# A decoder layer on one core: rows of b2 loaded ahead and the slot outputs read back in four parts

## What is computed

```python
dispatch = softmax(logits, axis=1)                      # logits (B, N, E, S) = (8, 512, 16, 16)
combine = softmax(logits.reshape(B, N, E * S), axis=-1).reshape(B, N, E, S)
slot_in = einsum('bnd,bnes->besd', xn, dispatch)
h = gelu(einsum('besd,edh->besh', slot_in, w1) + b1[None, :, None, :])
slot_out = einsum('besh,ehd->besd', h, w2) + b2[None, :, None, :]
out = einsum('besd,bnes->bnd', slot_out, combine)
x = layernorm(x + out)
```

## Time and profile before

| | |
|---|---|
| median of 3 runs | 2111.36 us (2105.56 to 2112.68) |
| the profiled execution's own time | 2112.64 us |
| its span | 2110.9 us |
| PE busy | 1974.6 us (94%) |
| DVE busy | 1453.8 us (69%) |
| ACT busy | 1221.2 us (58%) |
| mean over the span of what the DMA engines moved | 95 GB/s |
| expert loop, first output copy to last store landed | 2010.23 to 2051.62 us |
| combining, first to last DVE sum | 2055.65 to 2106.4 us |

### The profile page before, as it was taken

One profiled execution on the slowest core, in us unless ns is written; L12 is line 12 of the kernel. 1 busy time (PEld: TensorE's weight loads), 2 busy tenths in 40 slices (PEclk: granted clock), 3 DMA queues, 4 the chain that ended last, 5 costly groups with the idle time before them and its releaser, 6 DMA issues. The chain is left out here.

```text
span 2110.9 us, 40225 instructions
## 1 busy us (share of the span) xinstructions
PE 1974.6 (94%) x13484; PEld 1328.5 (63%) x13484; DVE 1453.8 (69%) x2889; ACT 1221.2 (58%) x3068; POOL 390.2 (18%) x597
## 2 busy tenths in 40 slices
PE   7899999999999999858999999999999999889988
PEld 5667675768676767444565656656656655478853
DVE  7978787878787878526667575757575767556438
ACT  4435353534444444217878787878787787546614
POOL 1110101111111111231221222222222122100006
PEclk9999999999999999878999999999999999999999
DMA  7122222222222222242324343433333332631157
GB/s 215 49 69 70 60 79 60 79 60 79 55 83 50 89 50 68 80 125 63 109 70 118 76 122 81 121 81 102 93 102 96 88 98 73 180 133 61 60 188 270
DMA packets 120291, 200.72 MB, mean 95 GB/s; under 512 B 23072, under 2 KB 44576, under 8 KB 120096
## 3 DMA queue, kind: packets, MB, share of 16 engines
q1 hardware_dynamic: 110880, 179.20, 28.3%
q0 software_dynamic: 9216, 18.89, 3.6%
HBM read 117.27 MB, written 29.88 MB: 70 GB/s over the span
## 5 line engine op out<-in xcount | busy, mean ns | idle before, releaser
L1769 ACT ACTIVATE a_shared<-a_shared,a_mx 128x512 f32<-128x512 f32 x512 | 340.9, 669 | 57.3 <-DVE a_mx L1830 57.2
L1762 ACT ACTIVATE a_probs<-a_scores 128x512 f32<-128x512 f32 x512 | 291.7, 603 | 98.8 <-PE a_scores L1972 96.4
L1830 DVE TENSOR_REDUCE a_mx<-a_shared 128x1 f32<-128x512 f32 x512 | 318.4, 682 | 14.4 <-PE a_shared L1956 13.3
L1972 PE MATMUL a_scores<-a_qs,a_ks 98*128 98x512 f32 x512 | 218.9, 435 | 21.7 <-ACT a_probs L1762 17.4
L1956 PE MATMUL a_shared<-a_ks,a_qs 96*128 96x512 f32 x512 | 214.9, 431 | 18.9 <-ACT a_shared L1769 14.3
L939 PE MATMUL m_proj<-m_xt_hi,link 128*128 128x512 f32 x544 | 224.6, 413 | 6.3 <-DVE m_acc L652 6.3
L1094 PE MATMUL m_outp<-m_wout,m_g 128*128 128x512 f32 x512 | 225.2, 598 | 2.7 <-issue 2.7
L940 PE MATMUL m_proj<-m_xt_lo,link 128*128 128x512 f32 x544 | 215.4, 396 | 0.0
L941 PE MATMUL m_proj<-m_xt_hi,link 128*128 128x512 f32 x544 | 214.3, 394 | 0.0
L1930 PE MATMUL a_shared<-link 128*128 128x512 f32 x768 | 190.6, 401 | 18.9 <-POOL a_ks L1702 15.7
L467 ACT ACTIVATE m_acc<-m_proj,m_cb,m_cw 128x512 f32<-128x512 f32 x72 | 58.1, 817 | 257.5 <-PE m_proj L941 257.3
(11 more groups left out here) (266 smaller groups left out, 3487.7 us busy)
## 6 DMA issues: line engine op xcount, KB each, us to landing
m_dec<-step_decay SPq DMA_DIRECT2D x64, 256.0 KB, 4.1
a_qs<-link SPq DMA_DIRECT2D x256, 64.0 KB, 2.1
m_ce<-run_decay SPq DMA_DIRECT2D x128, 112.0 KB, 3.5
a_ks<-a_k_hi POOLq DMA_DIRECT2D x192, 64.0 KB, 2.4
e_x<-x SPq DMA_DIRECT2D x11, 1024.0 KB, 5.6
m_xt_in<-x_t_in SPq DMA_DIRECT2D x8, 1024.0 KB, 8.3
m_x_tok<-x_in SPq DMA_DIRECT2D x8, 1024.0 KB, 5.5
x<-m_x_tok SPq DMA_DIRECT2D x32, 256.0 KB, 2.2
```

The costliest lines, as they stand in the source:

```text
L1762: act.activation(probs[:, n % 2, h, :], scores[t.score_bank(n, h)][:, :], ACT.Exp, scale=-1.0).then_inc(exp_ready, 1)
L1769: act.activation(scored[:, :], scored[:, :], ACT.Exp, scale=-1.0, bias=mx[:, i % 2, j, h:h + 1], accum_out=den[:, i, j, h:h + 1]).then_inc ...
L1830: dve.tensor_reduce(mx[:, i % 2, j, h:h + 1], bank(what)[:, :], AX.X, ALU.min).then_inc(mx_ready, 1)
L1972: pe.matmul(scores[t.score_bank(n, h)][:, :], ks[0:STACK + 2, t.slot(i), h, j * P:(j + 1) * P], qs[0:STACK + 2, t.slot(i), h, :], start=Tr ...
```

## The change

`b2row` now holds the rows of all eight experts 8 to 15, loaded at the stage's start in two DMAs of 1 MB, each with its own semaphore (`b2_in[0]`, `b2_in[1]`), and no row is loaded inside the loop. The 2 MB read of the first half becomes four of 512 KB, each for two sequences. They stand behind the stores of experts 9, 10, 11 and 12; the first still waits for the stores of experts 0 to 7. Each part has a semaphore of its own, three of them taken over from loads that are long done. VectorE waits for part n before it adds the bias to pair n.

```diff
-B_PAIR = 2
 HALF = NE // ST_TILES
-FIRST_ROW = HALF // B_PAIR
...
-        b2row = sb("b2row", [P, 2, B_PAIR, DM])
+        b2row = sb("b2row", [P, HALF, DM])
...
+        slot_in = [(c_in[0], 16), (b2_in[0], 32), (b2_in[1], 32), (b2_slot_in, 16 * HALF + 16)]
...
-            def load_bias(c):
-                sp.dma_start(b2row[:, c % 2], b2[B_PAIR * c:B_PAIR * (c + 1)].partition_broadcast(P)).then_inc(b2_in[c % 2], 16)
...
-            for c in range(FIRST_ROW, FIRST_ROW + 2):
-                load_bias(c)
+            for n in range(2):
+                half = slice(n * HALF // 2, (n + 1) * HALF // 2)
+                sp.dma_start(b2row[:, half, :], b2[HALF:NE][half].partition_broadcast(P)).then_inc(b2_in[n], 16)
...
-                if e >= HALF and e % B_PAIR == B_PAIR - 1 and e // B_PAIR + 2 < NE // B_PAIR:
-                    load_bias(e // B_PAIR + 2)
-                if e == HALF + 1:
+                piece = e - HALF - 1
+                if piece == 0:
                     for n in range(SO_BUFS):
                         sp.wait_ge(so_out[n], 16 * HALF // SO_BUFS)
-                    load_slots(0, 0, n_seq, c_in[0])
+                if 0 <= piece < n_seq // 2:
+                    s, count = slot_in[piece]
+                    if piece:
+                        sp.wait_ge(s, count - 16)
+                    load_slots(0, 2 * piece, 2 * piece + 2, s)
...
-                    c = e // B_PAIR
-                    dve.wait_ge(b2_in[c % 2], 16 * ((c - FIRST_ROW) // 2 + 1))
+                    dve.wait_ge(b2_in[2 * (e - HALF) // HALF], 16)
                     dve.tensor_tensor(so[0:rows, e % SO_BUFS, :], out_bank(e)[0:rows, :],
-                                      b2row[0:rows, c % 2, e % B_PAIR, :], ALU.add).then_inc(so_ready, 1)
+                                      b2row[0:rows, e - HALF, :], ALU.add).then_inc(so_ready, 1)
...
                     if b == 0:
-                        dve.wait_ge(c_in[0], 16)
                         dve.wait_ge(b2_slot_in, 16 * HALF)
+                    dve.wait_ge(*slot_in[b // 2])
```

## The result

Over 19 runs of each, the changed kernel took 2105.31 us (median; 2098.73 to 2109.71) and the one before 2111.66 us. The ratio is 0.9972, with a 95% interval of 0.9965 to 0.998: about 5.9 us less, 4.2 to 7.4. Its profiled execution has a span of 2105.0 us, against 2110.9.

The account below looks back on a forecast made before the run. For 24 us the end hung on transfers, with stores on half the DMA engines. The last store landing at 2046.3 instead of 2051.62 gains 5.3 us; less 0.3 for TensorE's clock, 5.0: from 2111.36 to 2106.4 us, gain 3 to 7 us.

Parts of the forecast that it names:

- L: Stretch from the issue of the first store to VectorE's first tile of the combining; 44.70 us in the kernel before.
- TensorE's clock: Late halves of the first sequences might start at 1.2 GHz; first tile up to 0.9 us later, 0.3 us taken.
- the end moves with the first tile: Combining: behind its first tile VectorE works 50.75 us without a break, so the end moves as much as that tile.
- The cost of nothing for the larger load: Stage start: 1 MB more of b2 rows, 2.6 us, hidden by 15.7 us of empty queue; cost 0.
- price of 2.56 us for a store and a part: Queue on the stores' engines: 1.24 us a store plus 1.32 us a 512 KB part, so each part lands 2.56 us later.
- Rival two: Every turn between store and read is slow, 4.0 us a pair; 2112.5 us; chance 0.16 with the cases between.
- the upper bound: Landing of the first part: at latest 2035.0, where the first b2 load landed; lower bound 2032.7, 2034.3 taken.
- the later of two ends: Last store lands 5.01 us after issue (2046.3) or when the queue behind the third part ends, 6.3 us (2045.7).
- the DMA share near 1 at first: Sign in the windows of the 8 us around the parts: share near 1 at first, never 0.5 for long.
- 0.7 + 1.3 us for a store and a part: Stores with 16 as slowest dimension: such a step hardly above TensorE's pace, saving near that of Rival one.
- Rival one: Parts hidden in full, experts keep TensorE's pace; everything moves by 9.4 us, to 2102.0; chance 0.12.
- chance of 0.34: Chance of being faster by over 0.3%, below 2105.0 us: Rival one and about a third of the forecast.

Follow-up runs that it names:

- e5: Changed kernel with VectorE's four bias adds moved behind expert 15's add; ratio 0.998, L 39.22 us.
- e8: Kernel before the change, only with stores on 16 DMA engines by the edit of e7; ratio 0.9981, L 40.81 us.
- e10: As e7 (stores on 16 engines, b2 rows ahead), but one read of 2 MB instead of four parts; ratio 0.9974, L 38.02 us.
- e7: Changed kernel with stores on 16 DMA engines, slots reordered where ScalarE writes them so the matmul reads contiguous data; ratio 0.996, L 34.82 us.
- e9: As e7, with the four bias adds also moved behind expert 15's add; ratio 0.9951, L 34.70 us.
- e6: Changed kernel with all four parts issued at once behind the store of expert 9; ratio 0.9978, L 39.74 us.
- e3: Changed kernel with stores on 16 DMA engines, the hidden layer's matmul reading with a 64-byte stride; ratio 1.0017, L 45.10 us.

## Why the prediction was right

The gain was forecast at 5.0 us, between 3 and 7, and measured at 5.9 us in the total and 5.4 in L. The mechanism held: the last store waits for a queue that the stores and the parts share. How near the sum came is in part luck, as the terms show.

Taken from the issue of the first store, so that the 0.49 us from the earlier stages are out, the terms compare as follows (predicted times are those of the prediction less 0.49).

| step | predicted | measured |
|---|---|---|
| part 0 lands, VectorE goes on | 2033.8 | 2033.64 |
| part 1 | 2036.4 | 2037.03 |
| part 2 | 2038.9 | 2039.58 |
| last add starts | 2040.1 | 2040.73 |
| last store goes out | 2040.8 | 2041.44 |
| it lands | 2045.8 | 2045.89 |
| TensorE's clock | + 0.3 | 0 |
| L | 39.7 | 39.34 |

**What bounds the kernel.** That the end moves with the first tile held: 55.25 us from it to the span's end before, 55.20 after, and VectorE waited for nothing behind it.

**The b2 rows.** The cost of nothing for the larger load held: 161.22 against 161.25 us from the stage's first load to the first store. The larger loads were not through by 1868 as before (the rate was still 94 GB/s from there to 1869 and 25 in the microsecond behind), but nothing waited for them.

**The parts in the queue.** The price of 2.56 us for a store and a part held for the steps from part 1 to 2 and from 2 to 3 (2.55 and 2.58); the step from part 0 to 1 took 3.39 us. The slow stretch at 218 GB/s (2028 to 2032), in which stores and reads are first mixed, lies ahead of part 0's landing, where the prediction had put it; from part 0 to part 1 the rate was 316 GB/s at a share of 0.86, so the 0.8 us are not that slow stretch. Rival two decided from 3.6 us for a pair on, and no step was that long. Part 0 landed 0.2 us ahead of the predicted time, which was chosen near the upper bound; that choice was right. The window between the two landings, and the one that the failed sign below is read from:

```profile
2033.64:2037.03 3.39, 2.01 (x6) 0.74 (x5) 1.83 (x3) 0.13 (x1) 0.00 (x0) 1.00 0.86 316
2036.00:2045.00 9.00, 7.67 (x18) 2.96 (x16) 4.88 (x5) 0.00 (x0) 0.00 (x0) 1.00 0.53 198
```

**The last store.** It took 4.45 us and not 5.01, which made up for the 0.6 us of the late parts. That these two errors are of opposite sign is luck, and it is why the sum is so near. The prediction had taken the later of two ends for this store: 5.01 us behind its issue, or 6.3 us of queue behind part 2. Measured, the queue's term holds (2039.58 to 2045.89, 6.31 us), and the 5.01 us does not act. So the queue sets the landing, as e5 shows too; in the prediction the 5.01 us hid that term.

**A sign that failed.** The prediction wanted the DMA share near 1 at first and never at 0.5 for long. It was 0.53 from 2036 to 2045, 9 us. Its own account asks for this: with the parts spread over 16 engines and the stores on 8, the other 8 run out of work first.

**The clock.** TensorE's clock was at 1.00 when the late products began, fell to 0.50 at 2049.9 and was back at 2053.3. TensorE had stood idle for 3.41 us ahead of them, against 4.3 predicted. VectorE lost nothing: its first two tiles start 1.62 us apart, as before the change (1.61). The prediction reads 3.20 us for four matmuls at 0.50, but there the clock was already 1.00 for the last part; four matmuls wholly at 0.50 took 3.62 us in e8, or 1.8 us for a tile, which is more than VectorE's 1.59. e8, and e10 by less, show that the term is real where the slow stretch falls on the early products.

**The limit.** The prediction put it in the 8 engines of the stores. The Trainium skill's rule (DMA: Bandwidth & Descriptors, on the increment by 16) gave the number, and the traces agree: in the changed kernel the share stays at 0.53 from 2036 to 2045 although stores and parts are queued, and with 16 as the slowest dimension stores alone take it up to 0.89 (e7). e7 and e8 change the slowest dimension and leave the bytes. They change the order of a store's rows with it, and no run changes one without the other. The last store's landing fell from 4.45 to 2.82 us behind its issue, and the queue's end from 35.4 to 30.7. The prediction's price for this case, 0.7 + 1.3 us for a store and a part, was too low: 2.7, 2.7 and 2.0 us were measured in e7.

Rival one, the parts hidden in full, fell with stores on 8 engines. With 16, L is 34.8, where it would be 44.7 - 9.4 = 35.3. That is near in the sum and not in its terms: in e7 the parts still hold VectorE, and the shorter last store makes up for it. Rival one was also worth 0.9 us more than I gave it, for at TensorE's pace the last expert's add stands only 0.86 us behind the one before it (e9). The chance of 0.34 for a gain above 0.3% was a fair statement of a result at 0.28%.

What stays open is why part 1 comes 3.39 us behind part 0. e6 issues the parts together and lands part 0 at 23.4 us, e10 lands the whole read earlier than I reckoned; neither takes this step apart. Nor do the totals tell e5, e6 and the changed kernel from each other, and the interval of e7's total still overlaps the changed kernel's; what sets e7 apart is L.

## What to carry to other kernels

Before splitting or moving a transfer, read what share of the DMA engines is busy while only one kind of transfer runs, and read it in short windows. The mean does not tell: it was 0.49 for the stores on 8 engines and 0.58 for those on 16. A share that no window of 1 us takes much above 0.5, even with several transfers queued, is that of a transfer that uses half of the engines, and a queue on that half delays whatever stands behind it, loads on all engines too. Cure the shape first: the same bytes with 16 as the slowest dimension were worth 3.9 us of L on the kernel before and 4.5 on the changed one, for five changed lines. And compare variants by the stretch that the edit touches, since the stages ahead of it moved the total by up to 6 us; but look at the end of the chain too, for in e5, e8, e9 and e10 TensorE and not the last transfer came last.

## What the runs showed of the hardware

- A matmul of 128x128x128 in float32 that reads its moving operand with a step of 64 bytes takes 395 ns in the profile instead of 275, and eight of them 1.74 us instead of 0.89.
- ScalarE's copy of 128x256 from PSUM takes 662 ns instead of 382 when it writes with a step of 32 bytes.
- The last store of 256 KB lands 2.8 us after its issue with 16 as its slowest dimension (e7, e3), 4.45 to 5.01 us with 8 (changed kernel, before), where part of the time is the queue ahead of it. With 16 and the queue full it took 4.96 us (e9).
- Four float32 matmuls of 128x128x512 take 3.62 us at a granted clock of 0.50 (e8) and 1.98 us at 1.00.
- A 512 KB load that repeats two rows of b2 on all partitions landed later than a read of 512 KB in the same place: 24.1 us after the first store's issue (2035.06) against 23.2, although it had been issued 0.8 us earlier. With stores on 16 engines it took 5.2 us from issue to landing (e8), the read 4.1 us (e7). What was queued behind them differs, so this is no clean comparison.
